# A vision-transformer layer kernel: the products of its attention part use all 128 rows and 128 columns of the TensorE array, small operands filled up with zeros

## What is computed

```python
h = tokens(x)      # sin and cos of 2 pi x f for 6 bands of f, 576 inputs each, times W: 6912 x 192
h = concat([cls_tok, h], axis=1)            # one more row for each image
h = h + attention(layernorm(h))
h = h + ffn(layernorm(h))                   # 8 experts, 2 a token, beside a shared one of width 768

def attention(x):                           # D = 192, M = 64
    q = (elu(x @ Wq) + 1) * 64 ** -0.5; k = elu(x @ Wk) + 1; v = x @ Wv
    c = clip(cumsum(log(sigmoid(x @ Wf + bf))), -20, 20)
    state = cumsum(exp(-c) * outer(k, v)); z = exp(c) * cumsum(exp(-c) * k)
    h = (q . (exp(c) * state)) / (q . z + 1e-6)
    return layernorm_with_gamma_beta(h) @ Wo
```

## Time and profile before

| | us |
|---|---|
| median of 3 runs | 567.93 |
| lowest, highest | 567.69, 571.91 |
| the profiled execution: its time | 567.73 |
| its span | 565.9 |
| TensorE busy in the span | 549.8 (97%) |
| VectorE, ScalarE, GpSimd busy | 368.6, 244.8, 175.0 |
| granted clock of TensorE, mean | 0.99 |

### The profile page before, as it was taken

The page is one execution under the profiler, slowest core; times in us unless marked ns, Lnnn a source line. Parts: engine busy times, 40 slices in busy tenths (PEclk is TensorE's granted clock), DMA queues, the critical chain, the costliest instruction groups (busy, mean ns, idle before and its releaser), DMA issues.

```text
span 565.9 us, 9023 instructions
## 1 busy us (share of the span) xinstructions
PE 549.8 (97%) x3235; PEld 506.0 (89%) x3235; DVE 368.6 (65%) x1060; ACT 244.8 (43%) x343; POOL 175.0 (31%) x200
## 2 busy tenths in 40 slices
PE   5999999999999999999999999999799999999997
PEld 5998999798999889999979999977688889999975
DVE  7636787534968636988852996467797446666537
ACT  3465373755225754343565422263233134454410
POOL 6412233113225311674312460002310504544410
PEclk9998999999999999999999999999898999999999
DMA  8900058000000000220000010510103251531164
GB/s 330 328 20 20 1 185 279 20 10 20 20 19 20 20 0 11 75 57 1 1 0 10 20 57 0 179 49 27 56 1 112 95 192 51 162 97 50 56 209 142
DMA packets 23488, 42.49 MB, mean 75 GB/s; under 512 B 2502, under 2 KB 15044, under 8 KB 23348
## 3 DMA queue, kind: packets, MB, share of 16 engines
q1 hardware_dynamic: 19560, 33.31, 18.1%
q0 software_dynamic: 3472, 8.07, 4.0%
q10 hardware_dynamic: 412, 0.53, 0.4%
HBM read 31.74 MB, written 14.79 MB: 82 GB/s over the span
## 4 chain that ended last, share of the span: by engine, by line
PE 88%; DVE 6%; ACT 3%; DMA 1%; issue 1%; POOL 0%; ACTq 0%; DVEq 0%
PE ps L1332 47%; PE ps L1534 5%; PE ps L1586 2%; PE ps L1588 2%; PE ps L1496 2%; PE ps L1498 2%; PE ps L1500 2%; PE ps L1499 2%; PE ps L1497 2%; PE ps L1564 1%; PE ps L1565 1%; PE ps L1566 1%; PE ps L1568 1%; PE ps L1567 1%; PE ps L1445 1%; PE ps L1361 1%
## 5 line engine op out<-in xcount | busy, mean ns | idle before, releaser
L1332 PE MATMUL ps<-w_tok,feat 128*128 128x192 f32 x1728 | 293.5, 331 | 7.5 <-ACT feat L479 6.2
L1332 PEld LDWEIGHTS ps<-w_tok,feat 128*128 128x128 f32 x1728 | 284.6, 192 | 11.8 <-issue 11.4
L413 POOL TENSOR_SCALAR feat<-fx 128x512 int32<-128x512 f32 x108 | 92.8, 874 | 198.7 <-PE ps L1332 195.1
L488 ACT ACTIVATE feat<-feat 128x1536 f32<-128x1536 f32 x35 | 51.9, 1484 | 112.4 <-DVE feat L781 112.3
L777 DVE SCALAR_TENSOR_TENSOR feat<-fx,feat 128x512 f32<-128x512 f32 x105 | 77.2, 788 | 2.0 <-POOL feat L413 1.5
L491 ACT ACTIVATE feat<-feat,half_pi 128x1536 f32<-128x1536 f32 x35 | 54.6, 1560 | 0.0
L449 POOL DMA_INDIRECT ydram<-yr,xs x39 | 37.3, 957 | 54.3 <-DVE yr L1102 54.3
L443 POOL DMA_INDIRECT slots<-pay_a,posi x17 | 17.6, 1034 | 75.7 <-DVE posi L1029 72.3
L781 DVE TENSOR_SCALAR feat<-feat 128x1536 int32<-128x1536 int32 x35 | 37.4, 1069 | 1.2
L1534 PE MATMUL ps<-w_down,hid_ring 128*128 128x192 f32 x192 | 37.2, 340 | 0.5 <-DVE H L1061 0.5
L592 ACT ACTIVATE s_ring<-ps 128x512 f32<-128x512 f32 x24 | 14.4, 598 | 53.7 <-PE ps L1500 53.7
(11 more groups left out here) (285 smaller groups left out, 853.9 us busy)
## 6 DMA issues: line engine op xcount, KB each, us to landing
slots<-in_blank SPq DMA_DIRECT2D x1, 5031.0 KB, 19.1
w_tok<-in_wT SPq DMA_DIRECT2D x7, 576.0 KB, 9.0
fx<-in_xT SPq DMA_DIRECT2D x15, 256.0 KB, 2.7
xs<-slots SPq DMA_DIRECT2D x5, 645.0 KB, 7.1
yin<-ydram SPq DMA_DIRECT2D x8, 384.0 KB, 7.2
raw_a<-in_wea SPq DMA_DIRECT2D x4, 384.0 KB, 5.6
raw_b<-in_web SPq DMA_DIRECT2D x4, 384.0 KB, 6.2
w_tok<-in_wT SPq DMA_DIRECT2D x4, 288.0 KB, 7.4
```

The source lines that it names most:

```text
L413: ins = pool.tensor_scalar(feat[:, k % SLOTS, i, :].bitcast(I32), x[:, x_block(k), :], f_col[:, fi:fi + 1], 1.0, ALU.mult, ALU.mult)
L488: act.activation(feat[:, k % SLOTS, 0:3, :], feat[:, k % SLOTS, 0:3, :], ACT.Sin, scale=TWO_PI).then_inc(sin_ready, 1)
L1332: ins = pe.matmul(ps[:, TOK[a % 2][t // 2], (t % 2) * D:(t % 2 + 1) * D], feat[:, k % SLOTS, i, t * P:(t + 1) * P], w_tok[:, k, i, :], sta ...
```

## The change

Every small product of attention 1 to 4 gets 128 rows: `wqk_b`, `wff_b`, `wv_b` and `wo_b` are read with all partitions (rows 0 to 63 of them are zeros in the packed input), and `xt_b` is a whole 128-row tile, in a new region `spare`, with zeros in its first 64 rows. Scores and q times state read all of `r`, in which rows 64 to 127 of the moved k, and of the states, are zeros. The transposes of k take in q as well (128 moving columns in place of 64), and ACT reads the k part of the result. The gain of the state has 128 weight columns, the last 64 of which nobody uses. For the class rows, transposes go through full 128x128 tiles whose other rows are zeros. Their products with two weight columns keep two. Ten memsets are new at DVE's start, ahead of the first features, and one later. `spare` lies where the unsplit shared weights were, and where image 3's router operands come later.

```diff
-        wqk_b, wff_b, wv_b, wo_b = (part(n, DB, P) for n in ("qk_b", "ff_b", "v_b", "o_b"))
+        wqk_b, wff_b, wv_b, wo_b = (part(n) for n in ("qk_b", "ff_b", "v_b", "o_b"))
...
+        with ExitStack() as fifth:
+            fifth.enter_context(nc.sbuf_tensor("pad_x", [P, 4 * T], F32))
+            spare = fifth.enter_context(nc.sbuf_tensor("spare", [P, 4, T], F32))
...
-        at = r[:, 0:4, 0:P]
-        k_rows = r[:, 0, P:P + (NT - 1) * M].rearrange("p (j m) -> p j m", m=M)
-        states = r[0:M, 1:NT, P:P + D + 1]
-        xt_b = r[DB:P, R_K, :]
+        k_rows = r[:, 0, P:NT * P].rearrange("p (j m) -> p j m", m=P)
+        states = spare[:, 2:4, :].rearrange("p i t -> p (i t)")[:, 0:(NT - 1) * (D + 1)].rearrange(
+            "p (j d) -> p j d", d=D + 1)
+        def at_of(a):
+            return r[:, R_E:R_E + 1, 2 * P:3 * P] if a == 0 else r[:, 0:4, 0:P]
+        def xt_b(a):
+            return r[:, R_P, :] if a == 0 else spare[:, 0, :]
...
-            return ps[0:M, (A1, A1, A0)[j], (j % 2) * (D + 1):(j % 2 + 1) * (D + 1)]
+            return ps[:, (A1, A1, A0)[j], (j % 2) * (D + 1):(j % 2 + 1) * (D + 1)]
...
-                act.activation(k_rows.rearrange("p j m -> p (j m)"), ps[:, A0, 0:(NT - 1) * M], ACT.Copy).then_inc(kt_ready, 1)
+                kt = ps[:, A0, 0:(NT - 1) * P].rearrange("p (j m) -> p j m", m=P)
+                act.activation(k_rows[:, :, 0:M], kt[:, :, M:P], ACT.Copy).then_inc(kt_ready, 1)
...
             dve.memset(one[:, :], 1.0)
+            dve.memset(v[:, 0, :], 0.0)
+            dve.memset(xn_c[:, :, :], 0.0)
+            dve.memset(pay_a[1][:, NT, :], 0.0)
+            dve.memset(r[0:M, R_P, 0:CLS], 0.0)
+            dve.memset(r[M:P, R_K, :], 0.0)
+            dve.memset(state[M:P, :], 0.0)
+            dve.memset(states[M:P, :, :], 0.0).then_inc(zeroed, 1)
+            dve.memset(r[:, R_E, P:3 * P], 0.0).then_inc(zeroed, 1)
+            dve.wait_ge(zeroed, 2)
+            dve.memset(r[0:1, R_E, P:2 * P], 1.0)
...
             attn8(0)
+            dve.wait_ge(split_done, SP_)
+            dve.memset(spare[0:DB, 0, :], 0.0)
             remainders(0, 8)
...
-                    pe.transpose(ps[:, A0, i * P:i * P + TP], xn_[0:TP, i, 0:P], ident[0:TP, 0:TP])
+                    pe.transpose(ps[:, A0, i * P:(i + 1) * P], xn_[:, i, 0:P], ident)
...
-                pe.matmul(ps[:, A0, 0:W], wff_b, xt_b[:, 0:W], start=False, stop=True).then_inc(f_psum, 1)
-                pe.matmul(ps[:, A2, 0:W], wqk_b, xt_b[:, 0:W], start=True, stop=False)
+                pe.matmul(ps[:, A0, 0:W], wff_b, xt_b(a)[:, 0:W], start=False, stop=True).then_inc(f_psum, 1)
+                pe.matmul(ps[:, A2, 0:W], wqk_b, xt_b(a)[:, 0:W], start=True, stop=False)
...
-                        ins = pe.transpose(ps[:, A0, j * M:(j + 1) * M], r[M:P, R_QK, j * P:(j + 1) * P], ident[M:P, M:P])
+                        ins = pe.transpose(ps[:, A0, j * P:(j + 1) * P], r[:, R_QK, j * P:(j + 1) * P], ident)
...
-                    ins = pe.matmul(score_place(j)[0:TP, 0:TP], r[0:M, R_K, c], r[0:M, R_QK, c], start=True, stop=True)
+                    ins = pe.matmul(score_place(j)[0:TP, 0:TP], r[:, R_K, c], r[:, R_QK, c], start=True, stop=True)
...
-                    pe.matmul(ps[0:M, A1, 0:D + 1], causal[0:1, 0:M], v[0:1, 0, :], start=True,
+                    pe.matmul(ps[:, A1, 0:D + 1], r[:, R_E, P:2 * P], v[:, 0, :], start=True,
...
-                        pe.matmul(place(i), r[0:M, R_QK, i * P:(i + 1) * P], state_at(i), start=(i % 2 == 0),
+                        pe.matmul(place(i), r[:, R_QK, i * P:(i + 1) * P], state_at(i), start=(i % 2 == 0),
...
-                    ins = pe.matmul(place(i), xt_b[:, i * P:i * P + TP], wo_b[:, :], start=False, stop=True,
+                    ins = pe.matmul(place(i), xt_b(a)[:, i * P:i * P + TP], wo_b[:, :], start=False, stop=True,
```

More of the change, by code:

```diff
@@ L157, in build @@
             raw_sb = fourth.enter_context(nc.sbuf_tensor("raw_sb", [P, NCS * 2 * P], F32))
+        with ExitStack() as fifth:
+            fifth.enter_context(nc.sbuf_tensor("pad_x", [P, 4 * T], F32))
+            spare = fifth.enter_context(nc.sbuf_tensor("spare", [P, 4, T], F32))
         X23 = sb("X23", [P, 2, 4, T], F32R)
         h_c = sb("h_c", [CLS, 1, D])
-        xn_c = sb("xn_c", [CLS, 1, D])
+        xn_c = sb("xn_c", [P, 1, D])
         xc = sb("xc", [P, 4, CLS], F32R)
         ht_cls = sb("ht_cls", [P, NCS * CLS])
-        state = sb("state", [M, D + 1])
+        state = sb("state", [P, D + 1])
         s_c = sb("s_c", [P, 1])
@@ L212, in build @@
         S = {n: sem(n) for n in names.split()}
-        (w_small, ws_in, wds_in, wde_in, cls_in, blank_in, split_hi, split_done, router_split, consts_ok,
+        (w_small, ws_in, wds_in, wde_in, cls_in, blank_in, split_hi, split_done, router_split, consts_ok, zeroed,
          n_first, r_first, sin_first, cos_first, wt_first, n_ready, r_raw, r_ready, sin_ready, tok_group,
@@ L806, in attn1 @@
                 dve.wait_ge(xpose1, a + 1)
-                dve.tensor_copy(xt_b[:, 0:W], ps[0:DB, A1, 0:W]).then_inc(xtb_ready, 1)
+                dve.tensor_copy(xt_b(a)[DB:P, 0:W], ps[0:DB, A1, 0:W]).then_inc(xtb_ready, 1)
             def negatives(a):
@@ L849, in attn3 @@
                 for j in range(nt):
-                    ins = dve.tensor_tensor(at[0:TP, j, 0:TP], score_place(j)[0:TP, 0:TP], causal[0:TP, 0:TP],
+                    ins = dve.tensor_tensor(at_of(a)[0:TP, j, 0:TP], score_place(j)[0:TP, 0:TP], causal[0:TP, 0:TP],
                                             ALU.mult)
@@ L855, in make_state @@
                 dve.wait_ge(state_psum, 1)
-                dve.tensor_scalar(state[:, :], ps[0:M, A1, 0:D + 1], r[0:M, R_K, 0:1], None,
+                dve.tensor_scalar(state[0:M, :], ps[0:M, A1, 0:D + 1], r[0:M, R_K, 0:1], None,
                                   ALU.mult).then_inc(state_ready, 1)
@@ L862, in add_states @@
                 for j in range(NT - 1):
-                    ins = dve.tensor_tensor(state_at(j + 1), gain_place(j), state_at(j), ALU.add)
+                    ins = dve.tensor_tensor(state_at(j + 1)[0:M], gain_place(j)[0:M], state_at(j)[0:M], ALU.add)
                     if j < NT - 2:
@@ L899, in attn6 @@
                 dve.wait_ge(xpose2, a + 1)
-                dve.tensor_scalar(xt_b[:, 0:W], ps[0:DB, A2, 0:W], gb_b[:, 0:1], gb_b[:, 1:2], ALU.mult,
+                dve.tensor_scalar(xt_b(a)[DB:P, 0:W], ps[0:DB, A2, 0:W], gb_b[:, 0:1], gb_b[:, 1:2], ALU.mult,
                                   ALU.add).then_inc(ntb_ready, 1)
@@ L1360, in values @@
                 for i in tiles_:
-                    ins = pe.matmul(place(i), xt_b[:, i * P:i * P + TP], wv_b[:, :], start=False, stop=True,
+                    ins = pe.matmul(place(i), xt_b(a)[:, i * P:i * P + TP], wv_b[:, :], start=False, stop=True,
                                     skip_group_check=True)
@@ L1416, in attn5 @@
                     for i in range(nt):
-                        pe.matmul(place(i), r[0:M, R_QK, i * P:(i + 1) * P], state_at(i), start=(i % 2 == 0),
+                        pe.matmul(place(i), r[:, R_QK, i * P:(i + 1) * P], state_at(i), start=(i % 2 == 0),
                                   stop=False, skip_group_check=True)
                 for i in range(nt):
-                    ins = pe.matmul(place(i), at[0:TP, i, 0:TP], v[0:TP, i, :], start=(nt == 1), stop=True,
+                    ins = pe.matmul(place(i), at_of(a)[:, i, 0:TP], v[:, i, :], start=(nt == 1), stop=True,
                                     skip_group_check=True)
@@ L1428, in attn6 @@
                 for i in range(nt):
-                    pe.transpose(ps[:, A0, i * P:i * P + TP], xn_[0:TP, i, 0:P], ident[0:TP, 0:TP])
+                    pe.transpose(ps[:, A0, i * P:(i + 1) * P], xn_[:, i, 0:P], ident)
                 for i in range(nt):
-                    ins = pe.transpose(ps[0:DB, A2, i * P:i * P + TP], xn_[0:TP, i, P:D], ident[0:TP, 0:TP])
+                    ins = pe.transpose(ps[0:DB, A2, i * P:(i + 1) * P], xn_[:, i, P:D], ident)
                 ins.then_inc(xpose2, 1)
@@ L1450, in attn8 @@
                 W, TP, nt = width(a)
-                pay_ = payload(a)
+                pay_ = pay_a[1][:, NT:NT + 1, :] if a == 0 else payload(a)
                 pe.wait_ge(xn2_ready, a + 1)
                 for i in range(nt):
-                    pe.transpose(ps[:, A2, i * P:i * P + TP], pay_[0:TP, i, 0:P], ident[0:TP, 0:TP])
+                    pe.transpose(ps[:, A2, i * P:(i + 1) * P], pay_[:, i, 0:P], ident)
                 for i in range(nt):
-                    ins = pe.transpose(ps[:, A1, i * P:i * P + TP], pay_[0:TP, i, P:XD], ident[0:TP, 0:TP])
+                    ins = pe.transpose(ps[:, A1, i * P:(i + 1) * P], pay_[:, i, P:XD], ident)
                 ins.then_inc(xpose3, 1)
```

4 lines of the change are left out of this document (2 added, 2 removed).

## The result

The changed kernel took 560.68 us (median, 558.78 to 560.72), the kernel before, in the same series, 569.05 us (567.69 to 571.91). The ratio is 0.9855, with a 95% interval of 0.9808 to 0.9901: faster by 1 to 2%. The forecast was 560.1 us, and its range of 557.3 to 562.9 holds the time.

What follows compares the result with a forecast made beforehand. TensorE, busy 97% of the span, was taken as the bound. Savings of 2.2 + 2.1 + 2.1 + 0.85 + 0.6 less 0.1 make 7.8 us, from the 567.93 median to 560.1 us; range 557.3 to 562.9.

Steps and rivals of the forecast that it cites:

- The size costs, 0.20 us a step: In TensorE's chain, each step from 128 rows to 64, or back, costs 0.20 us, paid by records behind it.
- Attention 1: 2.2 us: Steps gone in attn2 to attn7 save 2.2 us, counting attn2b's exit as lost and transposes of k as longer.
- Attentions 2 and 3: 2.1 each: Same steps as attention 1; about 0.7 of 0.8 us passes DVE's division, the rest waits at 1429: 2.1 us each.
- the rival in which the other engines hold on to 2.4 us: Attentions 1 to 3: savings after k's landing are waited off at 1417 and 1429 for DVE's normalization; 562.5 us, 12%.
- Attention 4: 0.85: Only savings before DVE takes over count, 0.60, 0.09 and 0.16 us; later ones are waited off: 0.85 us.
- the first term: Attention 4, before the chain leaves TensorE for ACT's copy of v: savings of 0.19 + 0.20 + 0.21 = 0.60 us.
- Attention 0: 0.6: Eight steps where TensorE bounds, 0.10 us each, less four transposes longer by 0.05: 0.6 us; the rest lost in waits.
- The start: 0.1 lost: Ten new memsets, 2.6 us, nearly covered by DVE's 2.56 us idle: delay 0.1 us, with 0 and 0.6 as ends.
- The widened weight loads: Rival at line 1399: 24 loads widened to 128 columns show by 53 ns each, 1.3 us; 561.4 us, 5%.
- the slower side: Rival: the gap belongs to lines such as 1371, 1361, 1417, 1445, not size, so padding leaves it; 568.8 to 569.3 us, 4%.
- That every step comes back: Rival, whole kernel: ACT and DVE lines move along, so all 56 steps of 0.20 us count; 11.2 us, 556.7 us, 10%.
- The clock rival: One more low-clock stretch, such as that behind the wait at 1429, makes 561.8 us, one fewer 558.4; 7%.

Runs made afterwards that it cites:

- the version where TensorE doesn't wait there: Changed kernel with the transposes of k and scores of attentions 1 to 3 placed 8 projection records later on TensorE: 558.63 us, ratio 0.9836 to the kernel before.
- the version with everything moved: Changed kernel with scores, DVE's expert-weight splits and zero fills later and the router cut in halves: 555.55 us, ratio 0.9766 to the kernel before.

## Why the prediction was right, step by step

- **The size costs, 0.20 us a step.** Right. Cutting the rows brings it back at those lines alone, cutting the columns at theirs, and a step made in the projections costs 0.40 in and out. The Trainium skill ("TensorEngine Tiling (Array Packing)", Key Properties) says that changing the tiling mode, and not only the tile, drains the engine; the traces agree in that the surplus of 0.15 to 0.20 us stands only where the size changes and 96 rows, more than half of the array, pay nothing. That it is a drain no trace shows, and why the transposes with 64 columns pay nothing stays open.
- **Attention 1: 2.2 us.** Measured 2.01. By the ends of the chain's pieces against the earlier trace rows, attn2 and attn2b gave 0.99 (0.80 + 0.21 forecast), nothing came from there to the landing of k, attn4 and attn5 with the exit of the scores 0.92 (0.96), attn7 0.39 (0.39). The step that was mis-sized is attn3: from the landing (127.60 before, 123.05 after) to the end of the scores it was 1.21 us and is 1.48, a loss of 0.27 where 0.15 was taken. The three longer transposes explain 0.15. The other 0.12 probably goes with the restart out of the wait, which was 0.13 us and is 0.34: the chain gives the three transposes 0.55 us behind it, and 0.33 in the version where TensorE doesn't wait there. No run separates it further.
- **Attentions 2 and 3: 2.1 each.** 1.97 and 1.99, with the wait at 1412 of 0.3 us or less in each and none at 1452. DVE's 0.46 us of room held, so the rival in which the other engines hold on to 2.4 us is out.
- **Attention 4: 0.85.** 0.77: from its first product of `attn2` to the transposes behind the wait it took 34.98 us (369.27 to 404.25), and takes 34.21 (362.93 to 397.14). The wait there is 3.7 us (3.6 to 3.9 forecast, 3.2 before), the one at 1477 0.3 (0.4 forecast). Moving DVE's splits shows that it was DVE's path. Inside, the first term came out smaller: from the first product to ACT's copy of v (0.60 forecast) it took 5.52 us and takes 5.07, for the chain now leaves TensorE at 360.84, ahead of `attn2`, for DVE's product at 1064. Some of what TensorE saves there shows as the wait at 1519, 0.8 us where it was 0.2.
- **Attention 0: 0.6.** From its first product of `attn2` to that of attention 1 the time fell by 2.18 us, of which one half-clock stretch at 46.09 of before is some 1.7: 0.5 is left. The two steps of its `attn1` lie ahead of that. From the kernel's first product to there it takes 1.46 us less, of which 1.29 is the full clock that comes earlier (below): 0.17 more, 0.65 in all.
- **The start: 0.1 lost.** The first remainder starts at 4.35 us, a little behind the 4.2 to 4.3 forecast, but so it does without the fills: POOL's rounding covers them, as the earlier trace rows suggested. The new memsets there are nine, not ten (DVE's ten more instructions count the later one too). In its own row a memset keeps the 0.83 ns an element, 485 and 541 ns for 512 and 579; together the nine move the memset behind them from 0.84 to 3.64, 2.80 us against 2.6 forecast and 2.74 of idle time. So the first product is 0.07 us later, within the scatter, and the delay of 0.6 us that a slower memset would have brought did not come.
- **Sum.** 2.01 + 1.97 + 1.99 + 0.77 + 0.65, less 0.07 at the start, is 7.3 us against 7.8 forecast and 7.0 between the profiled executions. Three more terms stand between. The full clock came at 9.38 us instead of 11.95 (half of 2.57, 1.3 us gained). Up to attention 4's transposes the changed kernel has two half-clock stretches (1.7 and 1.5) where the one before has one (1.7): 1.5 us lost. Behind them both take the same, 161.67 and 161.76 us, though the kernel before has two stretches there and the changed one only one: 0.1 us lost. What the missing stretch gives is waited off at 1557, where DVE sets the time. Its wait of 1.1 us stands in the eight profiled executions of all these kernels that have no half-clock stretch beginning between 415 and 431 us, and in none of the six that have one; the wait of 0.5 us behind it stands in all fourteen. This was not foreseen.
- **Luck.** The medians are 8.4 us apart, because two of the four executions of the kernel before took 570.18 and 571.91 us. The forecast of 560.1 is within 0.6 us of the time, but where the stretches fall and when the full clock comes are terms of 1.3 to 1.7 us each that the sum has at nothing, and here they nearly cancel. The parts above, and not the total, bear the prediction out.
- **The rivals.** The widened weight loads don't show (1422 adds 0.98 for six, had 189 ns a load). Padding left no step at its old price, so the slower side fell. That every step comes back fell at 1412 and 1452. The clock rival was right in kind: one stretch is 1.5 to 1.7 us, and it accounts for most of the spread of the changed kernel between 558.8 and 560.7, though one execution took 560.38 at the higher mean clock.

## What to carry to other kernels

Where products of 128 rows and columns alternate with smaller ones, compare what equal numbers of records add in the chain: a surplus of 0.2 us at the first group of another size, and again behind it, is the price of the passage (64-column transposes showed none), and zeros that fill the small ones up are free as long as the moving columns stay the same and the fill hides. What is saved counts only up to the next wait for another engine, so look for that wait first: here moving DVE's work out of one such wait was worth 2.9 us, about a third of the whole change. Before a gain of 1.7 us is put down to an edit, look at the granted clock by stretch in more than one execution.

## What the runs showed of the hardware that was not expected

- Ninety-six rows cost the same as 128 (7.80 us a step), 64 rows 0.40 and 64 columns 0.34 us more for one passage in and out.
- Half-clock stretches of 3.41 us (in four profiled executions one of 6.83) come in some executions of one and the same kernel and not in others, and not only behind waits: the one at 183.46 begins 60 us behind the last listed wait of TensorE, which is 100% busy in it. With 64-row products back there were four in both profiled executions, in the changed kernel three in one and a single longer one in the other, and in the version with everything moved none.
- A stretch at half clock can cost nothing where TensorE would otherwise wait for another engine: behind attention 4's transposes the kernel before took 161.67 us with two stretches, the changed one 161.76 with one and a wait of 1.1 us more.
